# Whole counts in two passes for the relational layers of a graph network

## The reference

```
h = concat(x, node_emb[node_type])                     # 768 + 128 features
xw = einsum('nd,rde->rne', h, w_rel)                   # a linear map per relation
count[v, r] = edges of relation r that end in v
agg[v] = sum over edges (u, v, r) of xw[r, u] / count[v, r]
h = relu(agg + h @ w_root + bias)                      # 896 -> 896 -> 768 -> 768
```

## Time and profile before

| | us |
|---|---|
| median of 3 runs | 1930.31 (1929.89 to 1932.41) |
| the profiled execution, whole | 1929.76 |
| its span, first to last instruction | 1928.0 |
| TensorE busy in the span | 1641.2 (85%) |
| VectorE, ScalarE, GpSimd busy | 762.1, 569.9, 515.1 |

### The profile page before, as it was taken

One profiled execution on the slowest core, in us unless ns is written; L12 is line 12 of the kernel. 1 busy time (PEld: TensorE's weight loads), 2 busy tenths in 40 slices (PEclk: granted clock), 3 DMA queues, 4 the chain that ended last, 5 costly groups with the idle time before them and its releaser, 6 DMA issues.

```text
span 1928.0 us, 27544 instructions
## 1 busy us (share of the span) xinstructions
PE 1641.2 (85%) x10719; PEld 1582.3 (82%) x10719; DVE 762.1 (40%) x1865; ACT 569.9 (30%) x1134; POOL 515.1 (27%) x669
## 2 busy tenths in 40 slices
PE   3977899897778889867999999999999997556786
PEld 2557889896768889857999999999999997556786
DVE  4985676314366662243311110101011113487633
ACT  2114443322244342122312122213121222355421
POOL 1014332332333332222222233223131222222121
PEclk7988998997889899978999999999999998776898
DMA  1112111122211111232111112111122222100012
GB/s 49 39 45 76 39 37 37 43 79 68 76 49 38 40 43 47 60 121 66 36 38 49 44 49 67 40 54 53 48 58 78 69 72 74 47 1 1 1 48 84
DMA packets 85289, 99.25 MB, mean 51 GB/s; under 512 B 8742, under 2 KB 77788, under 8 KB 85166
## 3 DMA queue, kind: packets, MB, share of 16 engines
q1 hardware_dynamic: 68660, 66.50, 12.0%
q10 hardware_dynamic: 16506, 31.07, 5.0%
HBM read 85.76 MB, written 11.77 MB: 51 GB/s over the span
## 4 chain that ended last, share of the span: by engine, by line
PE 64%; DVE 11%; issue 9%; ACT 6%; DMA 6%; POOL 3%; DVEq 0%; ACTq 0%; POOLq 0%; SPq 0%
PE ps L665 34%; PE ps L803 9%; PE ps L711 7%; PE ps L790 4%; PE ps L767 3%; PE ps L694 2%; DMA xl<-x_scratch 2%; PE ps L839 2%; DVE junk L1455 2%; DVE prob L1502 2%; PE ps L824 1%; DMA xl<-in_x 1%; POOL pairs L887 1%; DVE rl L1540 1%; ACT pairs L967 1%
## 5 line engine op out<-in xcount | busy, mean ns | idle before, releaser
L887 POOL TENSOR_TENSOR pairs<-stage,pairs 128x256 fp32r<-128x256 f32 (+3 forms) x472 | 367.7, 796 | 847.7 <-ACT pairs L967 846.5
L665 PE MATMUL ps<-pairs,XB 128*125 128x256 f32 (+1 forms) x2880 | 415.6, 307 | 24.3 <-POOL pairs L887 16.4
L665 PEld LDWEIGHTS ps<-pairs,XB 128*125 128x125 f32 x2880 | 408.6, 195 | 27.6 <-issue 13.0
L665 PE MATMUL ps<-pairs,XA 128*125 128x256 f32 (+2 forms) x2655 | 376.2, 303 | 6.9 <-DVE asp L1455 6.0
L665 PEld LDWEIGHTS ps<-pairs,XA 128*125 128x125 f32 (+1 forms) x2655 | 371.3, 189 | 9.2 <-DVE asp L1455 6.4
L967 ACT ACTIVATE pairs<-stage 128x256 fp32r<-128x256 f32 (+3 forms) x472 | 190.2, 425 | 580.8 <-PE ps L665 455.3
L711 PE MATMUL ps<-AT,Hg 125*128 125x314 f32 (+1 forms) x1080 | 169.0, 317 | 15.7 <-ACT asb L1101 7.2
L711 PEld LDWEIGHTS ps<-AT,Hg 125*128 125x128 f32 (+1 forms) x1080 | 163.3, 192 | 18.0 <-ACT asb L1101 8.1
L803 PE MATMUL ps<-MT,Hl 125*128 125x314 f32 x1170 | 171.9, 307 | 0.0
L803 PEld LDWEIGHTS ps<-MT,Hl 125*128 125x128 f32 x1170 | 170.2, 188 | 0.0
L1241 DVE TENSOR_TENSOR Hl<-ps,Hl 125x768 fp32r<-125x768 f32 (+3 forms) x57 | 43.6, 818 | 303.0 <-ACT Hl L1017 303.0
(11 more groups left out here) (149 smaller groups left out, 1570.2 us busy)
## 6 DMA issues: line engine op xcount, KB each, us to landing
stage<-in_W SPq DMA_DIRECT2D x192, 128.0 KB, 2.3
stage<-in_rel SPq DMA_DIRECT2D x99, 192.0 KB, 2.4
stage<-in_root SPq DMA_DIRECT2D x91, 64.0 KB, 1.8
x_scratch<-xo ACTq DMA_DIRECT2D x15, 375.0 KB
xl<-x_scratch ACTq DMA_DIRECT2D x15, 375.0 KB
stage<-in_rel SPq DMA_DIRECT2D x42, 128.0 KB, 2.1
stage<-in_root SPq DMA_DIRECT2D x12, 192.0 KB, 2.3
stage<-in_W SPq DMA_DIRECT2D x12, 192.0 KB, 2.4
```

Source lines behind the costliest of these rows:

```text
L665: last = mm(o, X[:rows, xi, a, P * (s0 + t):P * (s0 + t + 1)], pair(n, b), start=k == 0 and i == 0 and t * pitch % BANK == 0, stop=k == le ...
L887: nc.gpsimd.tensor_tensor(pair(n, 1), staged(n), pair(n, 0).bitcast(F32), ALU.subtract).then_inc(*up("weights_lo", "weights lo", n))
```

## The change

The transposed counts are no longer divided before the product. Whole numbers up to 4096 (`EXACT`) have no low half, so `MT` keeps one half only and the pass with its low half goes: two passes in place of three. The division comes afterwards, so each relation needs a sum of its own:

- Layers 1 and 2: the root product is a PSUM tile of its own, which ScalarE copies with the bias to `rl`. A step `relation_sum` for each relation fills another tile with 2 halves x 5 source tiles x 2 passes = 20 matmuls. VectorE multiplies it by a row of inverse counts (`degrees`) into `scaled` and adds that to `rl`. After the third, `pick_columns` fills two more columns, ScalarE clips into the high half, VectorE makes the low half.
- Layer 3: the root product stays in its five banks, each relation of a tile takes one of the three others, and VectorE adds each, scaled per target, to the row part. `norm_T` of the tile before stands behind `row_part` for every tile.
- Three steps `degrees` transpose the inverse counts into rows over all partitions.

A count above 4096 would not be exact. Two extra source columns, the clones, take what is beyond it: a step `repeats` finds which source nodes have such a count (the first and the last), the clones' features are copied through every layer by `pick_columns`, and the last source tile has 127 rows in place of 125. With the inputs of the reference no count is near that, and the clones' work is done all the same. `count_columns` takes the place of `mean_rows`.

```
+EXACT = 4096.0
+CLONES = 2
...
     yield chunk(0, 0)
+    if l == 0:
+        yield ("repeats",)
...
                 if i == 1 and c == 0:
+                    if r == 0:
+                        for k in range(R):
+                            yield ("degrees", k)
                     for d in range(NT):
                         yield ("mean_T", r, d)
             if i < 3:
                 for f in range(w // 128):
                     yield ("combine", i, c, f)
+                    for r in range(R):
+                        yield ("relation_sum", i, c, f, r)
...
+                elif kind == "relation_sum":
+                    _, i, c, f, r = s
+                    q = acquire(*s)
...
+                    for half in range(2):
+                        for t in range(NT):
+                            rows = P + CLONES if t == NT - 1 else P
+                            for a in range(2):
+                                last = mm(halves(q, 128)[:, half, :], Hl[:rows, t, r, a, 128 * f:128 * f + 128],
+                                          MT[:rows, r, t, HC * half:HC * half + HC],
+                                          start=t == 0 and a == 0, stop=t == NT - 1 and a == 1)
...
+                    if s[1] == 2:
+                        pe.wait_ge(*at("picks"))
+                        for k in range(6):
+                            c0 = 3 * P + 1 + CLONES * k
+                            last = mm(slot(q)[:, c0:c0 + CLONES], rows[:, 128 * k:128 * k + 128],
+                                      pickc[:, s[2], :], start=True, stop=True, skip_group_check=True)
...
+                    if r == R - 1:
+                        act.wait_ge(*at("stage sum", i, c, f))
...
+                        A(X[:, xi, 0, :], rl[:, n % 2, :], ACT.Relu).then_inc(*up("x2_hi", "stage hi", i, c, f))
...
+            def pick_columns(out_of, rows, n):
+
+                for j in range(CLONES):
...
+                    V.tensor_tensor_reduce(out=picked[:n, k % 2, :N], in0=rows, in1=pick[:n, j, :N], scale=1.0,
+                                           scalar=0.0, op0=ALU.mult, op1=ALU.add, accum_out=out_of(j)).then_inc(
...
+                    V.tensor_scalar(mean[:, d, :N], counts, EXACT, None, ALU.min)
+                    last = pick_columns(lambda j: column[:, d, j:j + 1], counts, P)
...
+                    V.tensor_tensor(h2(scaled[:, m % 2, :]), halves(q, 128), h2(degrees[:, r, :]),
+                                    ALU.mult).then_inc(*up("stage_step", "scaled", m))
...
+                    V.tensor_tensor(rl[:, n % 2, :], rl[:, n % 2, :], scaled[:, m % 2, :], ALU.add).then_inc(
+                        *up("stage_step", "added", m))
+                    if r == R - 1:
+                        dve.wait_ge(*at("added", m))
+                        last = pick_columns(lambda j: rl[:, n % 2, N + j:N + j + 1], rl[:, n % 2, :N], 128)
...
+                    for j in range(CLONES):
+                        V.tensor_scalar(pick[:, j, :], scaled[:, 0, :], pick_id[:, j:j + 1], None,
+                                        ALU.is_equal).then_inc(*up("embed", "pick rows", j))
...
+                    for r in range(R):
+                        qr = fill_of["combine_tile", c, d, r]
+                        dve.wait_ge(*at("part sum", c, d, r - 1))
+                        dve.wait_ge(*at("filled", "combine_tile", c, d, r))
+                        V.scalar_tensor_tensor(out=xh, in0=slot(qr)[:P, :384], scalar=inv[:, d, r:r + 1], in1=xh,
+                                               op0=ALU.mult, op1=ALU.add).then_inc(
```

More of the change, by code:

```diff
@@ L656, in _ @@
                                 n = first_tile[s] + k
+                                if g == len(gs) - 1 and k == 0 and s[:2] == ("relation", 1):
+                                    pe.wait_ge(*at("clones in"))
                                 if g == 0:
@@ L693, in _ @@
                     for j in range(NT):
-                        last = nc.tensor.transpose(slot(q)[:P, 128 * j:128 * j + P], M[:, d, P * j:P * j + P],
+                        m = P + CLONES if kind == "mean_T" and j == NT - 1 else P
+                        last = nc.tensor.transpose(slot(q)[:m, 128 * j:128 * j + P], M[:, d, P * j:P * j + m],
                                                    ident[:P, :P])
+                    last.then_inc(*up("psum_filled", "filled", *s))
+                elif kind == "degrees":
+                    q = acquire(*s)
+                    pe.wait_ge(*at("inverse degrees"))
+                    for j in range(NT):
+                        last = nc.tensor.transpose(slot(q)[:, 128 * j:128 * j + P],
+                                                   inv[:, j, s[1]:s[1] + 1].to_broadcast([P, 128]), ident[:P, :P])
+                    last.then_inc(*up("psum_filled", "filled", *s))
+                elif kind == "repeats":
+                    q = acquire(*s)
+                    pe.wait_ge(*at("ones"))
+                    for d in range(NT):
+                        pe.wait_ge(*at("repeats in", d))
+                        for c in range(2):
+                            last = mm(halves(q, 128)[:, c, :], ones16[:, :], repeats[:, d, HC * c:HC * c + HC],
+                                      start=d == 0, stop=d == NT - 1)
                     last.then_inc(*up("psum_filled", "filled", *s))
@@ L829, in _ @@
+                    G.same(("weights used", n), "filled", "rows", s, len(gs) - 1)
+                    for g, (s0, ns, pitch) in enumerate(gs):
+                        held.update(range(place[qs[g]], place[qs[g]] + ns * pitch // BANK))
                 elif kind == "combine_tile":
                     c, d = s[1:]
-                    g, t = d // 2, d % 2
-                    if d == 0:
-                        for r in range(R):
+                    if d in (2, 4):
+                        first_bank = place[fill_of["rows", ("combine_rows", c), d // 2 - 1]]
+                        held.difference_update(range(first_bank, first_bank + 2))
@@ L834, in _ @@
+                    for r in range(R):
+                        if d == 0:
                             pe.wait_ge(*at("rows lo", ("relation", 3, c, r, 384), 2))
[L835 to L836 removed]
+                        q = acquire("combine_tile", c, d, r, banks=1)
                         for u in range(NT):
[L838 to L840 removed]
@@ L841, in _ @@
-                    last.then_inc(*up("psum_filled", "filled", *s))
+                            rows = P + CLONES if u == NT - 1 else P
+                            for b in range(2):
+                                last = mm(slot(q)[:P, :384], MT[:rows, r, u, P * d:P * d + P],
+                                          Hl[:rows, u, r, b, :384], start=u == 0 and b == 0,
+                                          stop=u == NT - 1 and b == 1)
+                        last.then_inc(*up("psum_filled", "filled", "combine_tile", c, d, r))
@@ L844, in _ @@
+                    if d == NT - 1:
+                        held.clear()
         @block.sync
@@ new lines, in _ @@
+                    G.same(("scaled", m), "free", q)
+                    if r == 0:
+                        dve.wait_ge(*at("stage root", i, c, f))
+                    else:
+                        dve.wait_ge(*at("added", m - 1))
+                    dve.wait_ge(*at("scaled", m))
+                    V.tensor_tensor(rl[:, n % 2, :], rl[:, n % 2, :], scaled[:, m % 2, :], ALU.add).then_inc(
[3 more added lines that the diff above has]
+                        last = pick_columns(lambda j: rl[:, n % 2, N + j:N + j + 1], rl[:, n % 2, :N], 128)
+                        G.same(last, "stage sum", i, c, f)
+                        last_tile = (XB if i == 1 else XA, RGCN_CHUNKS[i][c][0] // 128 + f, 128, n % 2,
+                                     ("stage hi", i, c, f), ("stage lo", i, c, f))
@@ L1617, in _ @@
                         G.same(("part and bias", c, d), "free", q)
-                    dve.wait_ge(*at("part and bias", c, d))
+                    G.same(("part and bias", c, d), "part sum", c, d, -1)
+                    for r in range(R):
+                        qr = fill_of["combine_tile", c, d, r]
[3 more added lines that the diff above has]
+                                               op0=ALU.mult, op1=ALU.add).then_inc(
+                            *up("dve_step", "part sum", c, d, r))
+                        G.same(("part sum", c, d, r), "free", qr)
+                    dve.wait_ge(*at("part sum", c, d, R - 1))
                     dve.wait_ge(*at("x in", i))
```

259 lines of the change are left out of this document (189 added, 70 removed).

## The result

The changed kernel takes 1873.42 us (median of 4 runs, 1871.81 to 1874.38) against 1930.89 us of the kernel before in the same job: a ratio of 0.9701 (95% interval 0.9684 to 0.9718). That is 57.5 us faster, inside the range of 1852 to 1890, and 8 us above the predicted 1865.

The account below looks back on a forecast made before the run. The prediction took TensorE to bound the kernel, with no idle time where the diff works. From 1929.76 us, 81.6 off (56.6+25.0) and 16.6 on (6.4+5.3+1.2+3.7) gave 1865 us, eight times in ten 1852 to 1890.

Parts of the forecast that it names:

- Part 1: Layers 1 and 2: 90 matmuls per tile become 60, 56.6 us off; later weight splits at 8 turns, 6.4 on.
- The low end of the bound: Turns of layers 1 and 2: 0 us on if picks overlap, 27 if operations on SBUF inputs take 1.70 each.
- Part 2: Layer 3: 450 matmuls become 300, 25.0 us off over both chunks, the second limited by loads of x.
- fit under a tile of 5.3: Layer 3, first chunk: VectorE's bias, three sums and add, 3.0 us, hide under TensorE's tile; 13.3 us off.
- Tile 2 then has x at 4.4+0.3+9.0 = 13.7 us: Layer 3, second chunk: x load waits behind the normalisation's store and takes 9.0 us; 9.1 off, not 11.2.
- Part 3: Boundary to layer 1: VectorE's casts, masks and picks plus tiny fp32 matmuls delay the embedding; 5.3 us on (3 to 10).
- Part 4: Counts: column counting hides under projections, but three degree tiles join ScalarE's queue; 1.2 us on (0 to 4).
- Part 5: Start: extra count-tile operations and the repeats delay the scores TensorE waits for; 3.7 us on (1.5 to 8).
- (a): Sums run late: the queue reaches the turn, some 2.5 us at each of 8 turns; 1885, chance 0.19.
- (b): Everything hides: picks cost nothing, no x load is waited for, the start hides half; 1855, chance 0.12.
- (c): Slower by the clock: gaps at turns drop TensorE to 1.2 GHz, 2.6 us each fall; 1959, milder 1903; chance 0.04.
- (d): Weights bind: loads slow in layers 1 and 2, tiles stay 2 us longer, 26 us come back; 1891, chance 0.05.

Follow-up runs that it names:

- e10_embed_early: The boundary experiment: changed kernel with VectorE's embedding preparation moved into its idle times between block 1's last outputs, and GpSimd's number rows earlier; 1870.38 us.
- e8_half_load: Changed kernel with only columns 384 to 767 of x loaded in layer 3's second chunk; 1873.76 us.
- e3_hi_first: Changed kernel with ScalarE writing the high half of the previous tile's transposes before normalising the next tile, layer 3, second chunk; 1870.3 us.
- e9_all_half_load: Half load of x on top of the changed kernel with splits before the sum, high half before the normalisation and bias load early; 1858.64 us.

## Why the prediction was right, and where it was off

*Part 1* held. The pace is 0.145 us (60 in 8.88, with the pipeline's end), the tile distance fell by 4.35 us when the turn was mended (19.14 to 14.79), which is 30 x 0.145. The turn was predicted from rows for VectorE's four operations, 3.3 us from 988.17 to 991.5, and came so to a tenth; 8 x 0.8 were 8 x 0.90, and one turn was idle 0.97 us. GpSimd's weight half ended each wait, as said. Of what is left of the 2.0 us, 0.75 are in the four projections between the tiles, a term that the sum had at nothing: they took 37.32 and 56.64 us in place of 37.15 and 56.44 each. The low end of the bound (picks free beside GpSimd) was the right one: each took 0.81 and 0.82 at the turn. Where they do meet GpSimd, in `count_columns`, the same operation took 1.62 (899.10, in the boundary experiment, with GpSimd busy from 897.18 to 900.06); the rule of the Trainium skill that the prediction weighed (page "SBUF — State Buffer", section "Who interferes with whom") agrees with both, since GpSimd at the turn is itself waiting for ScalarE.

*Part 2* is the mis-sized term, 25.0 predicted and 14.9 in its two chunks. First chunk: 13.3 predicted, 9.1 measured (1426.01 to 1521.26, against 104.38 us before). The step that failed is "fit under a tile of 5.3": it costed VectorE's five operations and not the bias load that the first of them waits for, which the trace of before shows being issued 0.3 us after the first tile's start. The wait and the clock behind it are 3.8 of the 4.2 us. Second chunk: 11.75 predicted, 5.8 measured. The step that failed, "Tile 2 then has x at 4.4+0.3+9.0 = 13.7 us", made the load behind the store the bound of the chunk; that wait never came last, and so the sign "in the last chunk VectorE's addition of x waiting for the load" did not appear. The last tile's x was added 32.0 us after the first fill (1558.85 against 1526.81), not 26.55. What did come last was in the change's own text, as the step that puts `norm_T` of the tile before behind `row_part`: on ScalarE that is the high half behind the next normalisation, so that VectorE, which wants the high half before the next bias, adds its tile, the statistics, GpSimd's four operations and ScalarE's two into one loop of 8.7 us. I had summed VectorE's own work (5.5 us) and TensorE's (5.9), but not walked the chain across the engines. `e8_half_load` takes half of the load away and `e3_hi_first` the loop: the first brings nothing, the second 3.1, and the store is behind it. So the mechanism of this term was wrong, and not only its size.

*Part 3* held to 0.2 us. VectorE's added casts, masks and picks took 3.1 us (890.28 to 891.71 and 893.20 to 894.88; 3.2 predicted). The guess for the tiny matmuls, 1.5, was partly luck: they took 2.57 us at low clock (1.40 at full), but the transposes ahead of them ran in 1.02 us and not 1.49, so that both together ended 1.9 later. TensorE's idle time before the embedding itself grew by 3.6 us, not by the 5 given as a sign; the rest of the 5.4 is the time in which it worked on the tiny matmuls. *Part 4*: the second projection is 1.5 us later, as said (1.2), and the third another 0.9, since the 20 transposes from 945.44 and the projection behind them took 3.98 and 19.24 us. In the boundary experiment the same projection took 18.74 and the third followed the second by 23.61 us, not 24.75, so this is the clock and not the counting. The idle time ahead of it is not new: before the change gaps of 1.82 us stood in the same place twice (ahead of 914.11 and 937.93), and the 20 transposes behind them took 2.85 us each time. *Part 5*: the scores were 3.1 us late at 172.54 (3.7 predicted), but the prediction carried that to the end, and it doesn't get there: the shift is 1.5 at 450.62, 2.6 at 505.29, 0.2 at 818.17 and 0.5 at 884.34. That the attention blocks wait for loads and chains of their own, and that a late start shortens those waits, is how I read it; no run tests it, and 0.5 is less than what profiles of one program differ by there (882.45 to 885.40).

*The rivals.* (a), sums late at every turn by 2.5 us: no, no wait in the middle of a tile. (b), everything hides: in part. No x load was waited for and most of the start was hidden, two of its three conditions, but the turn cost stayed. (c), the clock: at the turns it stayed at 1.00 with gaps of 0.63 us, as forecast, but behind two single gaps, of 1.81 us (945.44) and 1.97 us (1433.43), it fell, and that cost 0.9 and 1.7 us. With the picks doubled it fell at two of eight gaps of 2.09. So falls came from a gap of 1.81 us on, near the lower end of the interval that I had named (1.06 to 6.27), and the length of the gap did not settle it. (d), the weights bind: no; the ring was ready wherever ScalarE was not held, and with the third pass back, in tiles 4.35 us longer, the turns still had the same waits of 0.60 to 0.62 us (one of 0.98). The time of 1873 lies between the forecast's 1865 and (a)'s 1885; only the trace says that (a) had no part in it.

## What to carry to other kernels

When the work between two events shrinks by a third, walk again through every load and every cross-engine chain that was hidden under it, the one-off loads (a bias) and the order of an in-order engine's steps above all; adding up each engine's own work finds neither. An engine that splits weights or feeds buffers should do that ahead of its wait for a late result: the same work cost 7 us here in one order and nothing in the other. And a delay early in a program should be carried to the end only after a look at the stretches between that wait for something else.

## What the runs showed of the hardware

A store of 125 rows of x to DRAM, 375 KB, was done 7.0 and 7.9 us after its issue in `e3_hi_first` (1531.31 to 1538.34, 1544.75 to 1552.60). With the load behind it halved, in `e9_all_half_load`, it was 6.9, 8.5 and 9.5 us, and the waits for it stayed (1.3 to 3.3 us). An fp32 matmul of two columns costs more than a transpose of 125: six of them, recorded as 12 instructions, took 1.40 us at full clock, against 0.80 for six transposes of 125 columns. TensorE's clock fell from 2.4 GHz behind gaps of 1.8 to 2.4 us in some cases and not in others. Of eight equal gaps of 2.08 or 2.09 us two were followed by slower matmuls (the rows of the double picks above), one of 12 matmuls in 3.48 us, one of 12 in 2.83; after the other six they took 2.00 to 2.02. At the wait for the bias the same 120 matmuls took 22.93 us behind a gap of 1.97 and 22.92 behind one of 2.39 (`e10_embed_early`), but without the picks and with the splits first they ran at full pace:

```profile
1424.60 21.39 PE L915 MATMUL ps<-Hl,MT 125*125 125x384 f32 x120 [2.31 <-DVE xo L1831]
1425.49 21.40 PE L915 MATMUL ps<-Hl,MT 125*125 125x384 f32 x120 [1.85 <-DVE xo L1835]
```

The granted clock of the 4 us from 1424 and from 1425 was 1.00 there, and 0.73 behind the gap of 1.97.
